# Two attentions of a language-model tower: query quarters, rings of three banks and a new order for the matmuls of a head

## The chip, the cores and the metric

One core of a Trainium2 chip runs the whole program as one launch. The metric is the device time in microseconds (us), the median of several executions. The core's engines run side by side, each on its own queue of instructions in order: TensorE (PE in the profile, with its weight loads as PEld), VectorE (DVE), ScalarE (ACT), GpSimd (POOL) and SyncE (SP), which here only issues DMAs. They meet at semaphores.

## The reference

The program is a tower of a token attention, a second attention with an extra term, a quantised feed-forward, a gated recurrence and six layers of local attention. The change lies in what the first two share. Cut to that (the token attention; the second one has temperature 1 in place of the scale, and adds three more features to the dot products):

```python
q, k, v = (split(q), split(k), split(v))          # 2 batches x 16 heads, 1024 tokens, 16 features a head
scores = jnp.einsum('bhqd,bhkd->bhqk', q, k) * scale
attn = jax.nn.softmax(scores, axis=-1)
ctx = jnp.einsum('bhqk,bhkd->bhqd', attn, v)
```

So there are 32 heads (a batch and a head together, `it` in the kernel) in each of the two attentions, and each has a score matrix of 1024 queries by 1024 keys.

## The kernel before

`softmax_attention` runs twice. `project` makes the queries and keys, splits them into a high and a low half, and writes them to a scratch tensor in HBM; `attend` does all 32 heads; then the output is transposed and projected. Inside `project`, before `attend`, GpSimd fills the value pads and the two rings `qs` and `ks` with constants (L323 to L332), while VectorE makes the scaled query bias `bqs` (L404), which ScalarE waits for before its first copy out of PSUM (L369, L379).

`attend` does a head in six pieces:

- SyncE loads `qs` and `ks` of a head into one of RING slots, 8 DMAs (L473).
- `score_for_max` (L493), 16 matmuls of 128 queries by 512 keys, one PSUM bank each. VectorE takes the maximum of each bank (`maximum`, L610) and then negates and joins them (L614).
- `max_row` (L501) transposes these maxima, 4 one-column transposes for each half of the queries, and ScalarE copies the row into partition 0 of `qs` (`take_row`, L572), so that the next matmuls subtract the maximum by themselves.
- `score` (L509), 16 matmuls of 128 keys by 512 queries; ScalarE takes the exponential of each bank into `probs` (L590).
- `weigh` (L521), in 4 groups a head: 4 matmuls of 32 weight columns by 512 queries, one key tile each, side by side in the four 32-column strips of the array. A half of the queries takes two groups. The four strips hold partial sums over different key tiles.
- ScalarE copies the 128 by 512 result (`take_output`, L578); `sum_groups` (L530), 4 matmuls with a constant matrix, adds the four strips and turns queries onto partitions; VectorE divides by the sums of the exponentials (`finish`, L620, L622).

The order of the work is written out by hand: a step of the PE queue works on the maxima of head `it + 1` and the scores of head `it` in turn, with the other pieces dropped in at fixed places (L544 to L563). The two kinds of matmul each have a ring of two PSUM banks. All engines run 4 steps unrolled, then a loop of 6 turns with 4 steps, then 4 steps unrolled.

## Time and profile before

| What | us |
|---|---|
| Median of 3 runs (4611.0 to 4611.99) | 4611.63 |
| The profiled execution | 4603.94 |
| Its span, first to last instruction | 4601.8 |
| First attention's heads, first maximum matmul to the next stage's first matmul | 123.02 to 617.69 |
| Second attention's heads, the same | 811.78 to 1305.06 |
| Mean granted TensorE clock | 0.962 |

The span is cut into stages in time: the two attentions with their projections fill the first 1310 us or so, and the six layers of local attention most of the rest. The time of a stage is read from its own window, not from the shares of the whole span. A row of a timeline gives the start in us, the duration in us, engine, line, operation and count; rows in one engine may be merged, and the idle time before them stands in brackets with what ended it. Matmuls are pipelined, so the time that one costs is the distance between the starts of neighbours and not its duration.

### The profile page before, as it was taken

To read this page: it belongs to the slowest core of one execution; us is meant where nothing else is said; L and a number is where in the kernel's file an instruction comes from. 1 tells how busy PE (TensorE), PEld (TensorE's weight loads), DVE (VectorE), ACT (ScalarE), POOL (GpSimd) and SP (SyncE) were. 2 spreads that over 40 slices of the span, in tenths; PEclk is the share of its full clock that TensorE was granted. 3 is DMA by queue.
4 is the path that set the end of the run, shared out by engine and by line. 5 is a ranking of instruction groups with operands and counts; after the bars stand their busy time and mean duration, and the time that the engine had idled before them with its cause. 6 is when DMAs were issued, how large, how long until landed. Compare 5 with 4: busy or idle time off the path is not lost. (4 is left out here: it accounts for less than half of the span.)

```text
span 4601.8 us, 97548 instructions
## 1 busy us (share of the span) xinstructions
PE 4219.3 (92%) x32438; PEld 2861.6 (62%) x32440; DVE 3251.8 (71%) x5725; ACT 2756.9 (60%) x7139; POOL 1931.9 (42%) x1276
## 2 busy tenths in 40 slices
PE   4999967999953579999999999999999999999997
PEld 2455543555531347777777777777777777777776
DVE  2677752777766767777777777777777777777775
ACT  1577723577723146666666666666666666666664
POOL 2000010000000056666666666666666666666663
PEclk9899988899977789999999999999999999999999
DMA  4211112211101120011100210011001110111001
GB/s 122 57 41 46 40 27 81 58 43 43 40 19 38 46 85 20 20 34 45 39 17 22 58 39 18 22 49 51 17 20 48 45 26 17 40 39 41 15 22 46
DMA packets 100922, 183.85 MB, mean 40 GB/s; under 512 B 24804, under 2 KB 58240, under 8 KB 100096
## 3 DMA queue, kind: packets, MB, share of 16 engines
q1 hardware_dynamic: 99712, 176.12, 14.3%
q8 instruction: 246, 4.03, 0.4%
q0 software_dynamic: 768, 2.10, 0.2%
q14 instruction: 196, 1.61, 0.1%
HBM read 99.52 MB, written 25.17 MB: 27 GB/s over the span
## 5 line engine op out<-in xcount | busy, mean ns | idle before, releaser
L610 DVE TENSOR_REDUCE maxima<-PS 128x1 f32<-128x512 f32 x1024 | 660.3, 687 | 242.6 <-PE PS L493 232.1
L1426 POOL TENSOR_TENSOR swp<-raw,table 128x512 f32<-128x512 f32 x384 | 481.3, 1274 | 635.8 <-DVE ss L1837 635.6
L1509 PE MATMUL PS<-wqk,xT 128*128 128x512 f32 x1536 | 688.0, 601 | 6.1 <-DMA wqk<-in_L_ffn_Wqkv 4.8
L590 ACT ACTIVATE probs<-PS 128x512 f32<-128x512 f32 x1024 | 551.8, 589 | 223.0 <-PE PS L509 218.5
L1456 POOL TENSOR_TENSOR probs<-probs,prob_recip 128x512 f32<-128x512 f32 x384 | 476.9, 1261 | 431.3 <-DVE prob_recip L1895 431.3
L1766 ACT ACTIVATE probs<-probs,neg 128x128 f32<-128x128 f32 x1536 | 597.1, 392 | 26.6 <-DVE neg L1889 25.1
L1436 POOL TENSOR_TENSOR rinv<-ssm,power 128x32 f32<-128x32 f32 x96 | 528.8, 5508 | 0.0
L493 PE MATMUL PS<-k_stack,q_stack 128*128 128x512 f32 x1024 | 466.6, 459 | 37.4 <-DMA k_stack<-L_attn_qk 17.7
L1509 PEld LDWEIGHTS PS<-wqk,xT 128*128 128x128 f32 x1536 | 284.3, 190 | 337.3 <-issue 254.1
L1612 PE MATMUL PS<-xnT,w 128*128 128x128 f32 x3840 | 477.6, 276 | 0.8 <-DVE hidden L1955 0.8
L482 POOL COPY v_head<-V 128x256 f32 (+1 forms) x64 | 25.4, 403 | 1041.7 <-PE PS L521 859.9
L1612 PEld LDWEIGHTS PS<-xnT,w 128*128 128x128 f32 x3840 | 452.8, 192 | 1.8 <-DVE hidden L1955 1.0
L1837 DVE TENSOR_REDUCE ss<-swp 128x16 f32<-128x1024 f32 x192 | 233.0, 1213 | 303.5 <-ACT swp L1717 303.5
L509 PE MATMUL PS<-q_stack,k_stack 128*128 128x512 f32 x1024 | 406.2, 399 | 2.6 <-ACT q_stack L572 1.4
L1716 ACT ACTIVATE raw<-PS 128x512 f32<-128x512 f32 x384 | 229.5, 598 | 282.6 <-PE PS L1509 278.8
L493 PEld LDWEIGHTS PS<-k_stack,q_stack 128*128 128x128 f32 x1024 | 196.5, 192 | 303.6 <-DVE maxima L610 248.5
L1591 PE MATMUL PS<-wo,oT 128*128 128x256 f32 x1536 | 347.4, 379 | 0.0
L1509 PE MATMUL PS<-wv,xT 128*128 128x512 f32 x768 | 345.8, 593 | 1.2 <-ACT swp L1717 1.2
L1880 DVE TENSOR_TENSOR probs<-PS,maskf 128x512 f32<-128x512 f32 x384 | 261.7, 681 | 101.5 <-PE PS L1553 101.2
L1591 PEld LDWEIGHTS PS<-wo,oT 128*128 128x128 f32 x1536 | 284.4, 190 | 34.7
L1739 ACT ACTIVATE kT<-PS 128x512 f32<-128x512 f32 x192 | 115.2, 600 | 309.5 <-PE PS L1527 309.5
L1901 DVE COPY pT<-PS 128x512 f32<-128x512 f32 x192 | 132.7, 691 | 230.4 <-PE PS L1562 230.1
(231 smaller groups left out, 8567.1 us busy)
## 6 DMA issues: line engine op xcount, KB each, us to landing
V_window<-V SPq DMA_DIRECT2D x180, 256.0 KB, 2.9
wqk<-in_L_ffn_Wqkv SPq DMA_DIRECT2D x12, 1024.0 KB, 6.8
w<-in_L_ffn_W SPq DMA_DIRECT2D x18, 640.0 KB, 4.4
q_stack<-L_tok_qk SPq DMA_DIRECT2D x128, 80.0 KB
k_stack<-L_tok_qk SPq DMA_DIRECT2D x128, 80.0 KB
q_stack<-L_attn_qk SPq DMA_DIRECT2D x128, 80.0 KB
k_stack<-L_attn_qk SPq DMA_DIRECT2D x128, 80.0 KB
wv<-in_L_ffn_Wqkv SPq DMA_DIRECT2D x6, 1024.0 KB, 5.1
```

The costliest lines, as they stand in the source:

```text
L493: pe.matmul(SM(k % 2), qs[:, r, (k // 2) * P:(k // 2 + 1) * P], ks[:, r, (k % 2) * CH:(k % 2 + 1) * CH], start=True, stop=True).then_inc(s ...
L509: pe.matmul(ST(k % 2), ks[:, r, (k % QT) * P:(k % QT + 1) * P], qs[:, r, (k // QT) * CH:(k // QT + 1) * CH], start=True, stop=True).then_i ...
L590: act.activation(probs[:, k % 8, :], ST(k % 2), ACT.Exp).then_inc(exp_done, 1)
L610: dve.tensor_reduce(maxima[:, par, k // 2, k % 2:k % 2 + 1], SM(k % 2), AX.X, ALU.max).then_inc(sm_maxed, 1)
L1426: pool.tensor_tensor(swp[:, w, :, a:a + LD // 2], raw[:, w, :, b:b + LD // 2], table[:, j % 2, 2 + w, a:a + LD // 2].rearrange("p (o d) -> ...
L1436: pool.tensor_tensor(rinv[:, :], ssm[:, :], power[:, :], ALU.pow).then_inc(S["inv_ready"], 1)
L1456: pool.tensor_tensor(view, view, psr[:, 4 * q:4 * q + 4].rearrange("p (h o) -> p h o", o=1) .to_broadcast([P, 4, P]), ALU.mult).then_inc(p ...
L1509: mm = pe.matmul(wide(kind, half, j), xT[:, k, at:at + P], rhs, start=(k == 0), stop=(k == DC - 1))
L1591: mm = pe.matmul(ATT, oT[:, j % 2, k * P:(k + 1) * P], wo[:, k, :], start=(k == 0), stop=(k == PAIRS - 1))
L1612: mm = pe.matmul(bank[:, at * P:(at + 1) * P], w1[:, w, k, f * P:(f + 1) * P], xnT[:, k, :], start=(k == 0), stop=(k == DC - 1), skip_grou ...
L1766: ins_ = act.activation(probs[:, h, :], src, ACT.Exp, bias=neg[:, h:h + 1], accum_out=psum_[:, h:h + 1])
L1880: dve.tensor_tensor(probs[:, 4 * q:4 * q + 4, :], SC(q % 2), maskf[:, int(j % QT == 0), :].rearrange("p (o k) -> p o k", o=1).to_broadcast ...
```

## The change

`attend` is rewritten around the same mathematics:

- `RING` is 6 in place of 4, so `qs` and `ks` have 6 slots each, and `project` fills the larger rings.
- `SM` and `ST` have three PSUM banks each in place of two. A maximum or score matmul waits for the third bank back instead of the second.
- `weigh` gives each of the four strips a quarter of the queries (256) and all key tiles. A burst is 4 key tiles by 4 quarters, 16 matmuls of 32 weight columns by 256 queries; a head has two bursts in place of four groups. Each strip then holds its whole sum, in one bank of 256 columns.
- `sum_groups` goes, and with it the constant `group_sum` and its DMA. `turn_output` takes its place: 2 transposes of 128 by 128.
- The maxima of a head are turned by one 8-column transpose; ScalarE copies 8 by 128 once a head, and SyncE moves it to partition 0 of `qs` with a DMA (`place_row`).
- VectorE does one join, one reciprocal and one multiplication a head in place of two of each.
- The order is new. A step now touches five heads: the maxima of heads `t` and `t - 1`, the scores of `t - 2` and `t - 3`, the weighing of `t - 3` and `t - 4`. There are 36 steps for 32 heads: 6 unrolled, 4 turns of a loop with 6, and 6 more unrolled.

The diff, cut to its core (the removed bodies are those quoted above; the other engines' loops change in the same way):

```diff
-RING = 4
+RING = 6
...
-    GROUP = 4
+    QUARTERS = 4
+    QW = SEQ // QUARTERS
+    BANKS = 3
     vh = c.sb(ctx, "v_head", [P, RING, QT, VW])
-    probs = c.sb(ctx, "probs", [P, 8, CH])
-    maxima = c.sb(ctx, "maxima", [P, 2, QT, 2])
+    probs = c.sb(ctx, "probs", [P, QT, SEQ])
+    maxima = c.sb(ctx, "maxima", [P, QT, HALVES])
     neg_max = c.sb(ctx, "neg_max", [P, 2, QT])
-    partial = c.sb(ctx, "partial", [P, 2, CH])
-    recip = c.sb(ctx, "recip", [P, 2, GROUP])
-    SM, ST, O = (lambda i: c.PS[:, i, :]), (lambda i: c.PS[:, 2 + i, :]), (lambda i: c.PS[:, 4 + i, :])
-    MR, CB = c.PS[0:1, 6, :], c.PS[:, 7, 0:GROUP * VW].rearrange("p (g v) -> p g v", g=GROUP)
+    neg_row = c.sb(ctx, "neg_row", [QT, 2, P], F32R)
+    partial = c.sb(ctx, "partial", [P, 2, QW])
+    recip = c.sb(ctx, "recip", [P, QT])
+    O, CB, MR = c.PS[:, 6, 0:QW], c.PS[:, 7, 0:QW], c.PS[0:QT, 7, QW:QW + P]
+    def SM(r, k):
+        return c.PS[:, (r + k) % BANKS, :]
+    def ST(r, k):
+        return c.PS[:, BANKS + (r + k) % BANKS, :]
...
+    MISC_JOBS = [("row", 1), ("turn", 4)]
+    MISC_TAKEN = {"row": row_taken, "turn": ctx_done}
+    def misc_free(pe, kind, it):
+        at = [k for k, _ in MISC_JOBS].index(kind)
+        t = it + MISC_JOBS[at][1]
+        for back in range(1, 4):
+            k, lag = MISC_JOBS[(at - back) % 2]
+            before = t - (0 if at >= back else (1 if at + 2 >= back else 2)) - lag
+            if not isinstance(it, int) or 0 <= before < ITERS:
+                wait(pe, MISC_TAKEN[k], before + 1)
+                return
+    def over_heads(eng, step, last):
+        for t in range(RING):
+            step(t, t, 0)
+        with eng.Fori(1, ITERS // RING) as turn:
             for u in range(RING):
-                step(turn * RING + u, u)
-        for it in range(ITERS - RING, ITERS):
-            step(it, it % RING)
+                step(turn * RING + u, u, turn)
+        for t in range(ITERS // RING * RING, ITERS + last):
+            step(t, t % RING, t // RING)
+    def stage(t, u, turn, lag):
+        if isinstance(t, int) and not 0 <= t - lag < ITERS:
+            return None
+        return t - lag, (u - lag) % RING, (turn if u >= lag else turn - 1)
...
+            def place_row(h):
+                it, r, turn = h
+                sp.wait_ge(row_taken, it + 1)
+                sp.dma_start(qs[0:1, r, :].rearrange("o (a t) -> o a t", a=QT).bitcast(F32),
+                             neg_row[:, r % 2, :].bitcast(F32)).then_inc(row_loaded[r], 16)
+            def step(t, u, turn):
+                h0, h3 = (stage(t, u, turn, lag) for lag in (0, 3))
+                if h3:
+                    place_row(h3)
+                if h0:
+                    load(h0)
+            over_heads(sp, step, 3)
...
+            def score_for_max(h, k):
+                it, r, turn = h
+                q, half = k // 2, k % 2
                 if k == 0:
-                    pe.wait_ge(loaded[r], (it - r) * (128 // RING) + 128)
-                wait(pe, sm_maxed, m - 1)
-                pe.matmul(SM(k % 2), qs[:, r, (k // 2) * P:(k // 2 + 1) * P], ks[:, r, (k % 2) * CH:(k % 2 + 1) * CH],
+                    pe.wait_ge(loaded[r], 128 * turn + 128)
+                wait(pe, sm_maxed, UNITS * it + k - BANKS + 1)
+                pe.matmul(SM(r, k), qs[:, r, q * P:(q + 1) * P], ks[:, r, half * CH:(half + 1) * CH],
                           start=True, stop=True).then_inc(sm_done, 1)
-            def max_row(it, r, half):
-                pe.wait_ge(neg_ready, 2 * it + half + 1)
-                wait(pe, row_taken, 2 * it + half)
-                for i in range(4):
-                    q = 4 * half + i
-                    mm = pe.transpose(MR[:, i * P:(i + 1) * P], neg_max[:, r % 2, q:q + 1], c.ident[:, :])
-                mm.then_inc(row_done, 1)
-            def score(it, r, k):
-                g = UNITS * it + k
-                if k % QT == 0:
-                    pe.wait_ge(row_taken, 2 * it + k // QT + 1)
-                wait(pe, exp_done, g - 1)
-                pe.matmul(ST(k % 2), ks[:, r, (k % QT) * P:(k % QT + 1) * P], qs[:, r, (k // QT) * CH:(k // QT + 1) * CH],
+            def max_row(h):
+                it, r, turn = h
+                pe.wait_ge(max_ready, it + 1)
+                misc_free(pe, "row", it)
+                pe.transpose(MR, neg_max[:, r % 2, :], c.ident[:, :]).then_inc(row_done, 1)
+            def score(h, k):
+                it, r, turn = h
+                if k == 0:
+                    pe.wait_ge(row_loaded[r], 16 * turn + 16)
+                wait(pe, exp_done, UNITS * it + k - BANKS + 1)
+                pe.matmul(ST(r, k), ks[:, r, (k // 2) * P:(k // 2 + 1) * P], qs[:, r, (k % 2) * CH:(k % 2 + 1) * CH],
                           start=True, stop=True).then_inc(st_done, 1)
-            def weigh(it, r, grp):
-                half = grp // 2
-                pe.wait_ge(exp_done, UNITS * it + 4 * grp + 4)
+            def weigh(h, grp):
+                it, r, turn = h
+                pe.wait_ge(exp_done, UNITS * it + 8 * grp + 8)
                 if grp == 0:
                     pe.wait_ge(v_taken, it + 1)
-                if grp % 2 == 0:
-                    wait(pe, o_taken, 2 * it + half - 1)
-                for j in range(4):
-                    kt = 4 * (grp % 2) + j
-                    mm = pe.matmul(O(half)[VW * j:VW * (j + 1), :], vh[:, r, kt, :], probs[:, 4 * (grp % 2) + j, :],
-                                   start=(grp % 2 == 0), stop=(grp % 2 == 1))
+                    wait(pe, o_taken, it)
+                for kt in range(4 * grp, 4 * grp + 4):
+                    for j in range(QUARTERS):
+                        mm = pe.matmul(O[VW * j:VW * (j + 1), :], vh[:, r, kt, :], probs[:, kt, j * QW:(j + 1) * QW],
+                                       start=(kt == 0), stop=(kt == QT - 1))
                 mm.then_inc(pv_done, 1)
...
+            def turn_output(h):
+                it, r, turn = h
+                pe.wait_ge(o_taken, it + 1)
+                misc_free(pe, "turn", it)
+                for i in range(2):
+                    mm = pe.transpose(CB[:, i * P:(i + 1) * P], partial[:, r % 2, i * P:(i + 1) * P], c.ident[:, :])
+                mm.then_inc(turned, 1)
+            def step(t, u, turn):
+                h0, h1, h2, h3, h4 = (stage(t, u, turn, lag) for lag in (0, 1, 2, 3, 4))
+                if h3:
+                    score(h3, 5)
+                if h1:
+                    score_for_max(h1, 8)
+                if h4:
+                    weigh(h4, 1)
...
+            def take_row(h):
+                it, r, turn = h
+                act.wait_ge(row_done, it + 1)
+                if not isinstance(it, int) or it >= 2:
+                    act.wait_ge(row_loaded[(r - 2) % RING], 16 * (turn if r >= 2 else turn - 1) + 16)
+                act.activation(neg_row[:, r % 2, :], MR, ACT.Copy).then_inc(row_taken, 1)
+            def take_output(h):
+                it, r, turn = h
+                act.wait_ge(pv_done, 2 * it + 2)
+                wait(act, turned, it - 1)
+                act.activation(partial[:, r % 2, :], O, ACT.Copy).then_inc(o_taken, 1)
+            def exponential(h, k):
+                it, r, turn = h
+                act.wait_ge(st_done, UNITS * it + k + 1)
+                if k % 8 == 0:
+                    wait(act, pv_done, 2 * (it - 1) + k // 8 + 1)
+                act.activation(probs[:, k // 2, (k % 2) * CH:(k % 2 + 1) * CH], ST(r, k), ACT.Exp).then_inc(exp_done, 1)
...
+            def maximum(h, k):
+                it, r, turn = h
+                dve.wait_ge(sm_done, UNITS * it + k + 1)
+                if k == 0:
+                    wait(dve, max_ready, it)
+                dve.tensor_reduce(maxima[:, k // 2, k % 2:k % 2 + 1], SM(r, k), AX.X, ALU.max).then_inc(sm_maxed, 1)
+            def row_maxima(h):
+                it, r, turn = h
+                dve.wait_ge(sm_maxed, UNITS * it + UNITS)
+                wait(dve, row_done, it - 1)
+                dve.tensor_reduce(neg_max[:, r % 2, :], maxima[:, :, :], AX.X, ALU.max, negate=True).then_inc(max_ready, 1)
+            def invert(h):
+                it, r, turn = h
+                dve.wait_ge(turned, it + 1)
+                wait(dve, ctx_done, it)
+                view = CB.rearrange("p (c g v) -> p c g v", c=2, g=QUARTERS)
+                dve.reciprocal(recip[:, :].rearrange("p (c g o) -> p c g o", c=2, g=QUARTERS), view[:, :, :, HD:HD + 1]).then_inc(ctx_recip, 1)
+            def finish(h):
+                it, r, turn = h
+                dve.wait_ge(ctx_recip, it + 1)
+                view = CB.rearrange("p (c g v) -> p c g v", c=2, g=QUARTERS)
+                out = context[:, :, bass.ds(it * HD, HD)].rearrange("p (g c) d -> p c g d", c=2)
+                by = recip[:, :].rearrange("p (c g o) -> p c g o", c=2, g=QUARTERS).to_broadcast([P, 2, QUARTERS, HD])
+                dve.tensor_tensor(out, view[:, :, :, 0:HD], by, ALU.mult).then_inc(ctx_done, 1)
...
```

What stands in PE's queue before, from the middle of a head in the unrolled start (L493 is a maximum matmul, L509 a score, L521 a weighing, L530 the sum over strips, L501 the transposes of maxima):

```order
L521 MATMUL PS<-probs,v_head 32x512 [waits exp_done_64]
L521 MATMUL PS<-probs,v_head 32x512 x3
L493 MATMUL PS<-k_stack,q_stack 128x512 [waits sm_maxed_59]
L509 MATMUL PS<-q_stack,k_stack 128x512 [waits exp_done_64,row_taken_62]
L493 MATMUL PS<-k_stack,q_stack 128x512 [waits sm_maxed_59]
L509 MATMUL PS<-q_stack,k_stack 128x512 [waits exp_done_64]
L530 MATMUL PS<-group_sum,partial 128x32 [waits ctx_done_69,o_taken_66]
L530 MATMUL PS<-group_sum,partial 128x32 x3
```

and now, in the first step that has all pieces (L539 is a maximum matmul, L553 a score, L564 a weighing burst):

```order
L539 MATMUL PS<-k_stack,q_stack 128x512 [waits sm_maxed_67]
L564 MATMUL PS<-probs,v_head 32x256 [waits exp_done_72]
L564 MATMUL PS<-probs,v_head 32x256 x15
L539 MATMUL PS<-k_stack,q_stack 128x512 [waits sm_maxed_67]
L553 MATMUL PS<-q_stack,k_stack 128x512 [waits exp_done_72]
L539 MATMUL PS<-k_stack,q_stack 128x512 [waits sm_maxed_67]
L553 MATMUL PS<-q_stack,k_stack 128x512 [waits exp_done_72] x2
```

The weighing matmuls of a head are 32 in place of 16, each half as wide, and they stand in two runs of 16 instead of four runs of 4.

The transposes of the maxima and the score that needs the row, now on PE (L546 is the one transpose, `row_loaded` the DMA's semaphore):

```order
L553 MATMUL PS<-q_stack,k_stack 128x512 [waits exp_done_72,row_loaded1_61]
L546 MATMUL PS<-ident,neg_max 8x128 [waits row_taken_70,max_ready_68]
L553 MATMUL PS<-q_stack,k_stack 128x512 [waits exp_done_72]
L539 MATMUL PS<-k_stack,q_stack 128x512 [waits sm_maxed_67]
```

The score waits here for the row of one head, and the transpose right behind it makes the row of the next, so the row has nearly a whole step to arrive. Before, the row of a head was copied in two halves inside the head's own step.

On VectorE, one head before (L610 the maxima, L614 the join, L620 and L622 the division):

```order
L610 TENSOR_REDUCE maxima<-PS 128x1 [waits row_done_61,sm_done_58]
L610 TENSOR_REDUCE maxima<-PS 128x1 [waits sm_done_58]
L620 RECIPROCAL recip<-PS 128x4 [waits sum_done_67]
L622 TENSOR_TENSOR context<-PS,recip 128x4x16 [waits ctx_recip_68]
L610 TENSOR_REDUCE maxima<-PS 128x1 [waits sm_done_58] x6
L614 TENSOR_REDUCE neg_max<-maxima 128x4 [waits sm_maxed_59]
```

and now (L705, L711, L718 and L726 in the same roles):

```order
L711 TENSOR_REDUCE neg_max<-maxima 128x8 [waits row_done_69,sm_maxed_67]
L705 TENSOR_REDUCE maxima<-PS 128x1 [waits max_ready_68,sm_done_66]
L705 TENSOR_REDUCE maxima<-PS 128x1 [waits sm_done_66] x5
L718 RECIPROCAL recip<-PS 128x8 [waits turned_75]
L705 TENSOR_REDUCE maxima<-PS 128x1 [waits sm_done_66] x2
L726 TENSOR_TENSOR context<-PS,recip 128x2x4x16 [waits ctx_recip_76]
```

The rows of before are half a head, those of now the first half of a step; the reciprocal waits for the two transposes of `turn_output`, with two maxima between it and the multiplication.

## Rows read from the trace of the kernel before

**Rows 1.** Window of 440 us: busy of PE, PEld, DVE, ACT, POOL, clock, DMA share, GB/s

```profile
160.00:600.00 440.00, 440.00 (x2594) 249.81 (x2592) 331.92 (x649) 310.72 (x590) 10.89 (x27) 1.00 0.16 41
```

**Rows 2.** Timeline of PE, first attention, half a head

```profile
401.08 0.40 PE L509 MATMUL PS<-q_stack,k_stack 128*128 128x512 f32 x1
401.40 1.07 PE L521 MATMUL PS<-probs,v_head 128*32 128x512 f32 x8
...
402.74 0.40 PE L509 MATMUL PS<-q_stack,k_stack 128*128 128x512 f32 x1
...
403.20 0.40 PE L509 MATMUL PS<-q_stack,k_stack 128*128 128x512 f32 x1
403.44 0.60 PE L501 MATMUL PS<-ident,neg_max 128*1 128x128 f32 x4
...
404.11 0.39 PE L509 MATMUL PS<-q_stack,k_stack 128*128 128x512 f32 x1
...
406.73 0.40 PE L509 MATMUL PS<-q_stack,k_stack 128*128 128x512 f32 x1
406.97 0.97 PE L530 MATMUL PS<-group_sum,partial 128*128 128x32 f32 x8
...
408.09 0.39 PE L509 MATMUL PS<-q_stack,k_stack 128*128 128x512 f32 x1
...
408.87 1.06 PE L521 MATMUL PS<-probs,v_head 128*32 128x512 f32 x8
```

**Rows 3.** Groups of instructions: busy us, mean ns of one, then idle before

```profile
L610 DVE TENSOR_REDUCE maxima<-PS 128x1 f32<-128x512 f32 x1024 | 660.3, 687 | 242.6 <-PE PS L493 232.1
L1591 PE MATMUL PS<-wo,oT 128*128 128x256 f32 x1536 | 347.4, 379 | 0.0
```

**Rows 4.** Timeline of PE in the local layers: 256-column matmuls back to back

```profile
2499.26 2.32 PE L1591 MATMUL PS<-wo,oT 128*128 128x256 f32 x10
```

**Rows 5.** Timeline of PEld: weight loads of one weighing group

```profile
401.40 0.16 PEld L521 LDWEIGHTS PS<-probs,v_head 128*32 128x32 f32 x8 [0.36 <-issue]
```

**Rows 6.** Timeline of PE in the local layers: strips of 64 columns, and transposes

```profile
2511.54 0.60 PE L1562 MATMUL PS<-ident,probs 128*128 128x128 f32 x4
...
2512.35 0.29 PE L1580 MATMUL PS<-pT,V_window 128*64 128x64 f32 x4
2512.47 0.29 PE L1580 MATMUL PS<-pT,V 128*64 128x64 f32 x4
```

**Rows 7.** Timeline of DVE, half a head

```profile
402.43 0.23 DVE L622 TENSOR_TENSOR context<-PS,recip 128x64 f32 x1
...
406.47 1.29 DVE L610 TENSOR_REDUCE maxima<-PS 128x1 f32<-128x512 f32 x2 [0.86 <-PE PS L493]
407.79 0.16 DVE L614 TENSOR_REDUCE neg_max<-maxima 128x4 f32<-128x8 f32 x1
```

**Rows 8.** Timeline of ACT, two exponentials

```profile
403.25 1.09 ACT L590 ACTIVATE probs<-PS 128x512 f32<-128x512 f32 x2
```

**Rows 9.** Timeline of PE: start and end of the heads of each attention

```profile
123.02 1.22 PE L493 MATMUL PS<-k_stack,q_stack 128*128 128x512 f32 x2 [16.57 <-DMA k_stack<-L_tok_qk]
124.60 1.39 PE L493 MATMUL PS<-k_stack,q_stack 128*128 128x512 f32 x2 [0.36 <-DVE maxima L610]
...
617.69 1.09 PE L165 MATMUL PS<-ident,context 128*128 128x128 f32 x4 [0.80 <-PEq L464]
...
811.78 1.22 PE L493 MATMUL PS<-k_stack,q_stack 128*128 128x512 f32 x2 [17.74 <-DMA k_stack<-L_attn_qk]
...
1305.06 1.17 PE L165 MATMUL PS<-ident,context 128*128 128x128 f32 x9 [0.80 <-PEq L464]
```

**Rows 10.** Timeline of POOL, DVE and ACT in the first projection

```profile
53.45 3.50 POOL L332 MEMSET k_stack<- 128x4096 f32 x1
...
46.48 10.50 DVE L404 TENSOR_SCALAR bqs<-bqk,factor 128x2 f32<-128x2 f32 x1 [2.26 <-POOL factor L326]
...
57.02 0.78 ACT L379 ACTIVATE whole<-PS,bqs,factor 128x512 f32<-128x512 f32 x1 [9.15 <-DVE bqs L404]
```

250 lines of the change are left out of this document (133 added, 117 removed).

## The prediction

> **What bounds the kernel now.** I read a window from the middle of the first attention first, then PE's timeline in it, and only then the other engines. In the window [rows 1] PE is busy for all of its 440 us at full clock (1.00), VectorE for 332 and ScalarE for 311, and DMA for 0.16. A busy PE proves little, since its records overlap, so the timeline has to say whether it ever waits. A weighing group starts at 401.40 and the one two places on, half a head later, at 408.87: 7.47 us a half, 14.94 a head. Priced by the starts of neighbours [rows 2]: two matmuls of scores or maxima lie between 402.74 and 403.20, so 0.23 each and 3.7 for the 16 of a half. From 401.08 to 402.74 stand two of them and a weighing group: 1.66 less 0.46 is 1.20, twice a half, 2.40. The four transposes of maxima: 403.20 to 404.11, less 0.46, 0.45. The sum over strips: 406.73 to 408.09, less 0.46, 0.90. Together 7.45 of 7.47. PE waits for nobody; a head costs what PE's queue costs, and every us taken out of that queue is one gained until VectorE or the rings get in the way.
>
> **The weighing.** A head now has 32 matmuls of 256 queries instead of 16 of 512, the same columns in all. The same moving size runs elsewhere: ten records of 256 columns take 2.32 us with 0.38 the mean of one [rows 3, 4], so (2.32 - 0.38) / 9 = 0.216 a record, and an fp32 matmul has two records. If the four strips run side by side, a burst is 4 key tiles x 2 x 0.216 = 1.73. The old group at that rate streams 2 x 0.43 = 0.86 of its 1.20; the other 0.34 is getting into and out of the strips, and is now paid twice a head instead of four times. So 2 x (1.73 + 0.34) = 4.14 against 4.80. The new part is that a strip needs fresh weights every 0.216 instead of every 0.43. Eight loads of a group occupy 0.16 in all, the second four beginning while the first matmuls run [rows 5], 0.08 a round; and in the local layers strips of 64 columns pass four matmul records in 0.12, each with a load of its own [rows 6]. I take the loads as hidden. Bounds: 1.73 below, and above, with every round showing its 0.08, 1.73 + 0.64 = 2.4 plus the 0.34.
>
> The Trainium skill (TensorE: Matmul & The Clock Gate, Measured speedup vs the span model) says that weight loads overlap with matmuls in flight only when the row group differs; all four strips here use all 128 rows, so by it the loads show and the upper bound holds. The trace disagrees: a score with its own 128-column load, on all rows too, still follows its neighbour after 0.23 [rows 2]. I keep a small chance for it below.
>
> **Transposes and the sum.** The four one-column transposes cost 0.45, 0.11 each [rows 2], and four full 128 by 128 transposes take the same 0.60 from first start to last end as those do [rows 2, 6], so I price both at 0.11. Before: 2 x (0.45 + 0.90) = 2.70 a head. Now one and two: 0.33. Upper bound 0.90, if the two transposes cost as much as the old sum.
>
> PE's queue for a head is then 32 x 0.23 + 4.14 + 0.33 = 11.8 to 11.9 (half-head prices are rounded), against 14.9.
>
> **VectorE and ScalarE.** Two maxima take 1.29 with 0.69 the mean of one, so the second starts 0.60 after the first [rows 3, 7]. Sixteen are 9.7; the join, of 0.16 [rows 7], waits for the last maximum and so costs some 0.3; a reciprocal and a multiplication, now once a head, some 0.5 (0.23 for the half-sized multiplication). That is 10.5, under PE's 11.9. Two exponentials take 1.09 [rows 8], 0.55 each at most, 8.8 a head, and two copies of 256 and 128 columns follow in place of four of 512: under 10.
>
> **The rings.** What decides between 11.9 and more is whether three banks carry VectorE over a burst and let PE run ahead after it. The nearest row: after a group of 1.20, with two banks, VectorE had been idle 0.86 [rows 7]. A burst is 0.87 longer and there is one more bank, worth 0.60: 1.13 idle a burst, so VectorE's own cycle would be 10.5 + 2 x 1.13 = 12.8 if the rings were always empty behind a burst. PE issues a maximum every 0.46 and VectorE takes one in 0.60, so after a burst PE gains 0.14 a pair and meets the end of the ring only after some four or five; then it waits a little. There are 7 pairs after one burst and 9 after the other. Between 11.9 and 12.8 I take 12.3 a head, nearer PE's sum because that sum met the kernel before to 0.02 us.
>
> **The row by DMA.** The row of a head is fetched nearly a step, some 11 us, before its score needs it, and SyncE's queue holds only the loads of a head three steps away ahead of it. I cost it at nothing. GpSimd's copy of the values waits for the second burst of a head six back; nothing waits for that.
>
> **Start and end.** Each attention's heads took 617.69 - 123.02 = 494.7 and 1305.06 - 811.78 = 493.3 [rows 9], 988.0 together. Now: steps 0 to 2 hold only 40 maxima (and five scores). At the start a pair of maxima took 1.58 (124.60 - 123.02, [rows 9]), 0.79 each, with PE waiting on VectorE's two banks; with three I take VectorE's own 0.60: 24 us, and 1 for joins (32 by the old rate). Then 29 full steps. Then the drain: step 32 has 24 matmuls and both bursts, 10; step 33 sixteen exponentials, 9; step 34 eleven and a burst, 8; step 35 a burst, a copy, two transposes and a division, 4: 31. Two more as an allowance for the first step that has scores in full. 25 + 29 x 12.3 + 31 + 2 = 415. Two attentions: 830, so 158 less.
>
> **What the larger rings cost.** GpSimd's fill of one ring takes 3.50 for 4096 columns [rows 10], and both grow by half: 3.5 us an attention. It is not hidden: VectorE's tiny scaling of the bias, 128 by 2, began at 46.48 and took 10.50, to within 0.05 of the end of the last fill (53.45 + 3.50), and ScalarE's first copy waits for it, idle 9.15 [rows 10]. Everything in the projection hangs on that copy. So 2 x 3.5 = 7 us come back. The Trainium skill (SBUF — State Buffer, SBUF: two separate sides) calls the port pair of VectorE and GpSimd an exclusive lock that the loser waits out. By that rule the wait would grow by the whole 3.5, and the row's 10.50 agrees.
>
> **Sum.** 158 - 7 = 151 off the profiled execution's 4603.9: 4453. The median of the runs shown is 7.7 above that execution; on its scale 4460.
>
> **Rivals.** (a) My forecast, PE's queue with small waits: 4460; its own range is 4437 (11.9 a head: 0.4 less in each of the 58 full steps) to 4489 (12.8). Chance 0.50. (b) The rings couple the engines: VectorE pays its 1.13 at each burst, and beside that waits about 0.5 for the two transposes of the output, which stand late in PE's step. 13.3 a head, 1.0 x 58 more: 4518. For it speak the 0.86 idle now and the reciprocal in the middle of eight maxima; against it PE's slack over VectorE. 0.30. (c) The page's rule on loads: eight rounds each show 0.08 more, 1.3 a head: 4535. Against it the 0.23 of a score. 0.05. (d) Slower: the strips don't stay side by side when 16 matmuls follow each other, and each of the seven changes of weights within a burst pays the entry of 0.34 again: 2.4 a burst, 4.8 a head, 278 us: 4738. It decides from 151 / 58 = 2.6 a head, 0.19 a change. No row shows two rounds with 32-column loads and 256 columns behind each other; rows 6 speak against it with 64-column strips. 0.08. (e) No change of note: the row's DMA or the loads arrive late, and a step waits its 14.9 out on them; about 4615. The loads keep a ring and DMA is busy 0.16 [rows 1]. 0.07, shared out between the smaller gains, no change and loss.
>
> **The numbers.** Faster by over 0.2% (9 us, about what can be told from no change): (a), (b), (c) and part of (e), 0.88. Within 0.2%: 0.03. Slower: 0.09. The range, 4425 to 4540, leaves out (d) and (e) and a few us below (a), where the fills stay hidden and the start is short.
>
> **What would show it.** Right: the weighing bursts two a head, 12.3 us apart from one head's first to the next's; the start of what follows a burst 2.1 after it; VectorE's scaling of the bias 3.5 longer; the rest of the program unmoved. Wrong by (b): PE's weight loads for the maxima idle on VectorE for more than 0.5 a head. Wrong by (c) or (d): bursts of 2.7 or more. Wrong by (e): the score after a row waits for the DMA.

## The result, and the profile after

| | before | after |
|---|---|---|
| Median, us | 4611.32 (4608.69 to 4611.99, 4 runs) | 4441.75 (4439.11 to 4443.88, 4 runs) |
| Ratio, 95% interval | | 0.9633 (0.9616 to 0.965) |
| Profiled execution, us | 4603.94 | 4443.18 |
| First attention's heads, us | 494.7 | 536.39 - 128.03 = 408.4 |
| Second attention's heads, us | 493.3 | 1143.60 - 735.01 = 408.6 |

3.7% faster; the forecast was 4460. The heads of both attentions give 988.0 - 817.0 = 171.0 us and the rest of the program takes back 10.2. The window of the heads, with the columns of [rows 1], and then the waits between 200 and 480 us (engine, line and what it waited for: total us, times, longest), both of the kernel after:

```profile
180.00:480.00 300.00, 300.00 (x2473) 192.58 (x2472) 255.10 (x475) 212.12 (x450) 9.67 (x24) 1.00 0.22 55
```

```profile
DVE maxima L705 <- PE PS L539: 40.9, 47, 1.0
...
PEld PS L553 <- ACT probs L669: 17.3, 90, 0.2
...
PEld PS L539 <- DVE maxima L705: 9.9, 24, 0.4
PEld PS L539 <- issue: 9.5, 23, 0.4
```

No single wait is longer than 1.0 us in these rows, and no row of PE's own queue waits for a transfer. The last two rows belong together: behind each of a head's two bursts the next weight load idles 0.4, at one burst put down to VectorE and at the other to nothing. PE's timeline for one head shows what the waits are worth (start us, duration us; a maximum matmul is L539 now, a score L553, a burst L564, the transpose of the maxima L546, those of the output L573):

```profile
301.79 0.40 PE L539 MATMUL PS<-k_stack,q_stack 128*128 128x512 f32 x1
302.12 1.93 PE L564 MATMUL PS<-probs,v_head 128*32 128x256 f32 x32
303.98 0.50 PE L539 MATMUL PS<-k_stack,q_stack 128*128 128x512 f32 x1
304.32 0.39 PE L553 MATMUL PS<-q_stack,k_stack 128*128 128x512 f32 x1
...
305.71 0.40 PE L553 MATMUL PS<-q_stack,k_stack 128*128 128x512 f32 x1
305.94 0.27 PE L546 MATMUL PS<-ident,neg_max 128*8 128x128 f32 x1
305.97 0.48 PE L553 MATMUL PS<-q_stack,k_stack 128*128 128x512 f32 x1
306.29 0.40 PE L539 MATMUL PS<-k_stack,q_stack 128*128 128x512 f32 x1
...
307.46 0.41 PE L553 MATMUL PS<-q_stack,k_stack 128*128 128x512 f32 x1
307.71 0.38 PE L573 MATMUL PS<-ident,partial 128*128 128x128 f32 x2
307.84 0.48 PE L539 MATMUL PS<-k_stack,q_stack 128*128 128x512 f32 x1
308.16 0.40 PE L553 MATMUL PS<-q_stack,k_stack 128*128 128x512 f32 x1
...
308.72 1.93 PE L564 MATMUL PS<-probs,v_head 128*32 128x256 f32 x32
...
308.72 1.45 PEld L564 LDWEIGHTS PS<-probs,v_head 128*32 128x32 f32 x32 [0.29 <-ACT probs L669]
```

Read by starts, as [rows 2] were: six steps from 304.32 to 305.71 are 1.39, 0.23 each, as before. A burst costs 304.32 - 301.79 = 2.53 less two steps, 2.06. The row's transpose costs 306.29 - 305.71 = 0.58 less two steps, 0.11; the two of the output 308.16 - 307.46 = 0.70 less two, 0.24. Over the window the bursts start 6.61 and 5.42 apart in turn, 12.03 a head. I call the 6.61 from the burst in the middle of a step (behind tile 15 of the maxima) to the one near the start of the next (behind tile 8) the long stretch; PE's sum in it is 18 x 0.233 + 2.06 + 0.35 = 6.60. The short stretch has 14 x 0.233 + 2.06 = 5.32 in 5.42.

VectorE in the same head (idle time in brackets, L705 a maximum, L711 the join, L718 and L726 the division), where [rows 7] had 0.86 idle behind a group of 1.20:

```profile
303.41 0.17 DVE L711 TENSOR_REDUCE neg_max<-maxima 128x8 f32<-128x16 f32 x1
304.52 3.68 DVE L705 TENSOR_REDUCE maxima<-PS 128x1 f32<-128x512 f32 x6 [0.93 <-PE PS L539]
308.12 0.21 DVE L718 RECIPROCAL recip<-PS 128x8 f32<-128x8 f32 x1
308.25 1.26 DVE L705 TENSOR_REDUCE maxima<-PS 128x1 f32<-128x512 f32 x2
309.43 0.28 DVE L726 TENSOR_TENSOR context<-PS,recip 128x128 f32 x1
...
311.12 4.28 DVE L705 TENSOR_REDUCE maxima<-PS 128x1 f32<-128x512 f32 x7 [0.82 <-PE PS L539]
```

Between bursts it never stops. It idles 0.82 and 0.93 behind the two bursts, and 12.03 less that is 10.3 of work. So two limits may hold this kernel, and they read almost the same: PE's sum, 11.92, and VectorE's work plus what a burst starves it of. The second comes to 12.03 by construction, since work and idleness together always fill the head, so it proves nothing by itself. The experiments turn on which of the two holds.

A third engine leaves a trace in the short stretch. Three score matmuls a head wait there with their weight load for a bank that ScalarE still reads, and PE's steps at them are 0.52 for two, 0.25 and 0.27 where they are 0.23 elsewhere (starts 312.31, 312.83, 313.07, 313.32, 313.54, 313.81); that is about the 0.1 between 5.32 and 5.42. One of the three:

```profile
312.49 0.19 PEld L553 LDWEIGHTS PS<-q_stack,k_stack 128*128 128x128 f32 x1 [0.22 <-ACT probs L669]
```

Start and end of the heads, and the fills ahead of them, which answer to [rows 9] and [rows 10]:

```profile
128.03 0.79 PE L539 MATMUL PS<-k_stack,q_stack 128*128 128x512 f32 x1 [17.26 <-DMA k_stack<-L_tok_qk]
...
536.39 3.87 PE L164 MATMUL PS<-ident,context 128*128 128x128 f32 x32 [0.90 <-PEq L492]
...
735.01 0.79 PE L539 MATMUL PS<-k_stack,q_stack 128*128 128x512 f32 x1 [17.76 <-DMA k_stack<-L_attn_qk]
...
1143.60 0.52 PE L164 MATMUL PS<-ident,context 128*128 128x128 f32 x3 [0.89 <-PEq L492]
...
50.77 5.21 POOL L330 MEMSET q_stack<- 128x6144 f32 x1
55.92 5.21 POOL L331 MEMSET k_stack<- 128x6144 f32 x1
...
47.25 13.91 DVE L403 TENSOR_SCALAR bqs<-bqk,factor 128x2 f32<-128x2 f32 x1 [2.26 <-POOL factor L325]
...
588.52 15.69 DVE L403 TENSOR_SCALAR bqs<-bqk,factor 128x2 f32<-128x2 f32 x1
```

The scaling went from 10.50 to 13.91 us, and still ends with the last fill (55.92 + 5.21 = 61.13, against 61.16). The heads start 5.0 later in the first attention, the stretch from the first attention's end to the second's start is 4.5 longer (194.1, now 198.6), and the rest grows by 0.9.

### The profile page after: what moved, and what is told of

The parts are those of the page before. It is cut to its first block and busy times, and to the rows that moved or that the text cites. A ratio compares the mean times of both kernels' runs of the same rounds, so it can differ in the third digit from the quotient of the medians.

```text
span 4441.2 us, 98171 instructions
## 1 busy us (share of the span) xinstructions
PE 4048.9 (91%) x33142; PEld 2813.6 (63%) x33144; DVE 3197.5 (72%) x5533; ACT 2627.5 (59%) x7011; POOL 1930.9 (43%) x1276
## 5 line engine op out<-in xcount | busy, mean ns | idle before, releaser
L705 DVE TENSOR_REDUCE maxima<-PS 128x1 f32<-128x512 f32 x1024 | 631.6, 680 | 129.9 <-PE PS L539 129.5
L669 ACT ACTIVATE probs<-PS 128x512 f32<-128x512 f32 x1024 | 519.2, 602 | 153.8 <-PE PS L553 153.3
L539 PE MATMUL PS<-k_stack,q_stack 128*128 128x512 f32 x1024 | 428.1, 438 | 36.4 <-DMA k_stack<-L_attn_qk 17.8
L553 PE MATMUL PS<-q_stack,k_stack 128*128 128x512 f32 x1024 | 392.1, 413 | 2.2 <-ACT probs L669 2.2
L1882 ACT ACTIVATION_READ_ACCUMULATOR probs<-probs,neg 128x1 f32 x1536 | 286.9, 187 | 0.0
```

The source lines that it names most:

```text
L539: pe.matmul(SM(r, k), qs[:, r, q * P:(q + 1) * P], ks[:, r, half * CH:(half + 1) * CH], start=True, stop=True).then_inc(sm_done, 1)
L553: pe.matmul(ST(r, k), ks[:, r, (k // 2) * P:(k // 2 + 1) * P], qs[:, r, (k % 2) * CH:(k % 2 + 1) * CH], start=True, stop=True).then_inc(st ...
L669: act.activation(probs[:, k // 2, (k % 2) * CH:(k % 2 + 1) * CH], ST(r, k), ACT.Exp).then_inc(exp_done, 1)
L705: dve.tensor_reduce(maxima[:, k // 2, k % 2:k % 2 + 1], SM(r, k), AX.X, ALU.max).then_inc(sm_maxed, 1)
L1882: ins_ = act.activation(probs[:, h, :], src, ACT.Exp, bias=neg[:, h:h + 1], accum_out=psum_[:, h:h + 1])
```

## The experiments

Theories. A: TensorE's queue of 11.92 sets the head, and waits add little. C: VectorE sets it, through the three banks of its ring. Where a later run asks for one stretch or one ring, A is called Q and C is called V; S is ScalarE through the exponentials' ring, E both engines level. L: the fills hold VectorE's bias scaling until the last one ends; W: something else sets its end; R: moved fills hold VectorE elsewhere instead. Medians are compared with 4441.8 for the kernel after; "heads" is the mean time of one attention's heads in the profile, 408.5 for it (first maximum matmul to the next stage's first matmul; in the experiments, to the last multiplication of the output, 408.15 for it).

**Is the burst what I priced?** Each burst is cut in two with a score or maximum matmul between the parts:

```
-                for kt in range(4 * grp, 4 * grp + 4):
+                for kt in range(4 * grp + 2 * part, 4 * grp + 2 * part + 2):
...
                 if h1:
                     score_for_max(h1, 9)
+                if h4:
+                    weigh(h4, 1, 1)
...
                 if h0:
                     score_for_max(h0, 0)
+                if h3:
+                    weigh(h3, 0, 1)
```

> The kernel after, with each burst of 16 weighing matmuls cut into two of 8, with one maximum matmul between them: four bursts of two key tiles a head in place of two bursts of four. Theory A (PE's queue sets a head, and each burst costs 0.33 us for entering and leaving the strips): 2 x 0.33 us x 62 heads or so, 41 us more, 4483 us. Theory C (VectorE's idle time behind long bursts sets a head): shorter bursts are kinder to the rings, so less than 10 us more, or less than the kernel after.

4482.82 us (4480.28 to 4486.68), ratio to before 0.9728 (0.9712 to 0.9744): 41.1 slower than after. PE's timeline:

```profile
309.86 1.07 PE L565 MATMUL PS<-probs,v_head 128*32 128x256 f32 x16
310.86 0.49 PE L539 MATMUL PS<-k_stack,q_stack 128*128 128x512 f32 x1
311.28 1.07 PE L565 MATMUL PS<-probs,v_head 128*32 128x256 f32 x16
```

A part and the matmul behind it take 311.28 - 309.86 = 1.42. Two key tiles are four records of 0.216 in each strip, 0.87 with the strips side by side; a step is 0.23; 0.32 is left for entering and leaving. The price of 0.34 an entry holds, and with it rival (d) falls: seven changes of weights inside a burst cost nothing.

**One PE cost doubled in the long stretch.**

```
-                for i in range(2):
+                for i in (0, 1, 0, 1):
                     mm = pe.transpose(CB[:, i * P:(i + 1) * P], partial[...
```

> The kernel after, with the two 128 by 128 transposes of the output done twice into the same place, 4 in place of 2 a head. Theory A (PE's queue sets a head): two more transposes of 0.11 us for each of 64 heads, 14 us more, 4456 us. Theory C (the rings and VectorE set a head, PE has air): 0 to 3 us more, 4442 to 4445 us.

4455.64 us (4452.54 to 4456.46), ratio 0.9667 (0.9651 to 0.9683): 13.9 slower. The long stretch is 6.81 instead of 6.61, the short one still 5.42. 0.20 of the 0.24 shows, as A says. Alone this doesn't decide, because the two transposes more also hold VectorE, whose reciprocal waits for them. In the kernel after they end at 307.71 + 0.38 = 308.09, just as VectorE is through its six maxima; here VectorE is through at about 305.54 + 6 x 0.60 = 309.14 and the transposes end at 308.72 + 0.60 = 309.32:

```profile
305.54 3.68 DVE L705 TENSOR_REDUCE maxima<-PS 128x1 f32<-128x512 f32 x6 [0.94 <-PE PS L539]
309.35 0.21 DVE L718 RECIPROCAL recip<-PS 128x8 f32<-128x8 f32 x1
```

So VectorE's cycle grew by 0.2 too. That PE is full in the long stretch is shown by its starts, 6.60 by the sum in 6.61, more than by this run.

**One VectorE cost added, in the short stretch and then in the long one.** A maximum more a head over one bank (128 by 512), at tile 12, and in the second kernel at tile 4:

```
+                if k == 12:
+                    wait(dve, spare_done, it)
+                    dve.tensor_reduce(spare[:, 0:1], SM(r, k), AX.X, ALU.max).then_inc(spare_done, 1)
```

> The kernel after, with one more maximum of a bank on VectorE for each head, into a spare tile, between the twelfth and the thirteenth of a head: 0.60 us more VectorE work a head, nothing more on PE. Theory A (PE's queue of 11.9 us sets a head of 12.02, VectorE has about 1 us of air, but the rings hold only three banks of it): 0 to 0.3 us a head more, 4442 to 4460 us. Theory C (VectorE's cycle sets a head): the whole 0.6 us a head, 38 us more, 4480 us.

> The changed kernel with one more maximum over a 128x256 score tile on VectorE in every head (its result goes to a spare tile and is not used), as in the run before it of this kind, but at key tile 4 of the scan, in the stretch of 6.6 us from the burst in the middle of a step to the burst at the start of the next, and not at key tile 12, in the stretch of 5.4 us behind it, where it cost 37.7 us. Theory A, each stretch has its own bound: in the longer stretch TensorE's queue of 18 matmuls, a burst and three transposes is full (6.6 by the sum of its steps, 6.61 measured) and VectorE has nine maxima, the row's maximum and the two operations on the output there, 6.1 us, with some 0.5 to spare; the 0.61 us of another maximum are hidden but for 0 to 0.1 a head: 4442 to 4450, and the shorter stretch stays at 5.42. Theory C, VectorE through the three-bank ring sets the pace all round: +0.6 a head as at key tile 12, 4480.

At tile 12: 4479.47 us (4478.37 to 4480.32), ratio 0.9718 (0.9702 to 0.9734), 37.7 slower; short stretch 5.97, long 6.60. A, as I held it then, missed by 19 us or more and C was right. I tried to save A by giving each stretch its own bound, and the run at tile 4 contradicts that too: 4477.92 us (4475.96 to 4478.46), ratio 0.9718 (0.9703 to 0.9733), 36.1 slower; long stretch 7.16, short 5.42. The first row is PE's timeline at tile 4, the others VectorE's:

```profile
303.25 0.50 PE L540 MATMUL PS<-k_stack,q_stack 128*128 128x512 f32 x1 [0.17 <-DVE maxima L709]
...
299.52 2.48 DVE L709 TENSOR_REDUCE maxima<-PS 128x1 f32<-128x512 f32 x4 [0.94 <-PE PS L540]
301.92 0.68 DVE L708 TENSOR_REDUCE spare<-PS 128x1 f32<-128x512 f32 x1
...
306.67 4.27 DVE L709 TENSOR_REDUCE maxima<-PS 128x1 f32<-128x512 f32 x7 [0.82 <-PE PS L540]
```

The idleness behind the bursts stays at 0.94 and 0.82: it isn't slack that more work could fill. It is the time of a burst that three banks don't bridge, so it belongs to VectorE's cycle. Each stretch grew by 0.55 for a maximum of 0.60. So in the kernel after VectorE was some 0.05 short of setting either stretch: about 5.37 and 6.56, 11.93 a head, an estimate from these two runs, beside PE's 11.92. Neither engine has room worth the name in the long stretch.

**A PE cost in the short stretch.**

```
                 wait(pe, sm_maxed, UNITS * it + k - BANKS + 1)
+                if k == 12:
+                    pe.matmul(SM(r, k), qs[:, r, q * P:(q + 1) * P], ks[:, r, half * CH:(half + 1) * CH],
+                              start=True, stop=True)
```

> The changed kernel, in which TensorE computes the score tile of key tile 12 of the scan twice into the same bank, one matmul more of 0.23 us a head, in the stretch of 5.42 us from the burst at the start of a step to the one in its middle, where TensorE's own steps sum to 5.32. Twice as many output transposes in the other stretch cost 13.9 us, 0.22 a head, and one maximum more cost 38 us in either stretch. Theory Q, TensorE's queue binds here too: +0.23 a head, 14 to 15 us, 4456. Theory V, in this stretch VectorE through its ring of three banks is 0.1 behind TensorE, and the first 0.1 of the matmul fills that wait: +0.13 a head, 8 us, 4450.

4455.3 us (4453.53 to 4457.98), ratio 0.9667 (0.9654 to 0.968): 13.5 slower, which is Q's number. The profile says otherwise: the bursts of the short stretch lie 5.57 apart, not 5.42, the long stretch is unchanged, and the heads grow by 4.8 and 4.1 us, 8.9 in all, which is the size that V gave. What is over lies between the attentions in the profiled run (2.9) and behind the second (1.1), where nothing was changed; from the last multiplication of the one to the first maximum matmul of the other, the nine profiles in which the fills stand as in the kernel after, this one among them, read 196.6 to 201.9. V's mechanism does not hold, though. With PE's waits for ScalarE's and for VectorE's banks in the same 280 us, and VectorE behind the burst in the middle of a step:

```profile
PEld PS L556 <- ACT probs L672: 9.0, 50, 0.2
...
PEld PS L542 <- DVE maxima L708: 9.5, 23, 0.4
...
305.95 3.68 DVE L708 TENSOR_REDUCE maxima<-PS 128x1 f32<-128x512 f32 x6 [1.09 <-PE PS L542]
```

The scores' waits for ScalarE fell from 90 to 50 and from 17.3 us to 9.0, those for VectorE stayed (9.9, now 9.5), and VectorE's idleness grew from 0.93 to 1.09, by what the stretch grew. So the added matmul went into the time that PE had spent waiting for ScalarE, and VectorE had a little room in the short stretch. No run here changes ScalarE's work, so its share of the 0.1 rests on these rows.

**Which banks carry it?** First two banks for either ring, with the order and the bursts of the kernel after:

```
-    BANKS = 3
+    BANKS = 2
...
-        return c.PS[:, (r + k) % BANKS, :]
+        return c.PS[:, k % BANKS, :]
...
-        return c.PS[:, BANKS + (r + k) % BANKS, :]
+        return c.PS[:, 3 + k % BANKS, :]
```

> The kernel after, with two PSUM banks in each of the two rings in place of three; the order and the bursts of 16 stay. Theory A (PE's queue of 11.9 us sets a head, and three banks are what lets it): with two banks VectorE is idle 0.86 us behind a burst of 1.2 in the kernel before, so 0.87 more behind a burst of 2.07: 10.5 + 2 x 1.73 = 14.0 us a head, or a little more, since the order has two matmuls of one kind behind each other: about 2.0 to 2.4 us x 58 more, 4557 to 4580 us. Theory B (the gain is the shorter PE queue alone, the third bank is not needed): 12.0 us a head, 4442 us.

4639.08 us (4636.9 to 4640.68), ratio 1.0064 (1.0048 to 1.0081): 197 slower than after, slower even than before, and 59 above the top of what I expected. Then one ring at a time, here the maxima's four and the exponentials' two (the second kernel has two and three, by the same places):

```
-        return c.PS[:, (r + k) % BANKS, :]
+        return c.PS[:, k % 4, :]
...
-        return c.PS[:, BANKS + (r + k) % BANKS, :]
+        return c.PS[:, 4 + k % 2, :]
...
-                wait(pe, sm_maxed, UNITS * it + k - BANKS + 1)
+                wait(pe, sm_maxed, UNITS * it + k - 4 + 1)
...
-                wait(pe, exp_done, UNITS * it + k - BANKS + 1)
+                wait(pe, exp_done, UNITS * it + k - 2 + 1)
```

> The changed kernel with the six score banks shared out otherwise: four for the tiles whose maxima VectorE takes, two for the tiles whose exponentials ScalarE takes (three and three in the changed kernel; two and two made it 197 us slower). What is open is which of the two rings that loss came from, and whether VectorE's 0.8 to 0.9 us of idleness behind each burst is what holds the head at 12.02. Theory V, the maxima's ring: with four banks VectorE has 0.6 us more to do during a burst, its idleness falls to about 0.3, and TensorE's queue alone sets the head at 11.9: 4435 to 4442. Theory S, the exponentials' ring: two banks make each score wait for the exponential two tiles back (some 0.4 for the matmul, 0.5 for the exponential and 0.1 between them, against a pitch of 0.47 in TensorE's order), and the waits behind the bursts come on top; then most of the 197 us are here: 4600 to 4640. Both alike: 4530 to 4560.

> The changed kernel with two banks for the tiles whose maxima VectorE takes and three for the exponentials' (two and two made it 197 us slower). Theory V, the maxima's ring carries the loss: VectorE idles 1.3 to 1.5 us behind each burst instead of 0.82 and 0.93, and TensorE waits for it at the other tiles: 4600 to 4640. Theory S, the exponentials' ring carries it: 4442 to 4480, of which 1.2 us a head less idleness hidden would be the most. Both alike: 4530 to 4560.

| Banks, maxima / exponentials | Median, us | Ratio to before, 95% | Long and short stretch, us | Heads, us |
|---|---|---|---|---|
| 3 / 3, after | 4441.75 | 0.9633 (0.9616 to 0.965) | 6.61, 5.42 | 408.2 |
| 4 / 2 | 4563.71 | 0.9904 (0.9889 to 0.992) | 7.63, 6.32 | 468.6 |
| 2 / 3 | 4582.81 | 0.9942 (0.9927 to 0.9957) | 8.10, 6.16 | 479.5 |
| 2 / 2 | 4639.08 | 1.0064 (1.0048 to 1.0081) | 8.47, 6.51 | 504.8 |

Neither V nor S: each ring alone, one bank short, costs 122 or 141 us, and both short cost 197. "Both alike" was right in kind, and 4 to 23 us low. With four and two, the scores' waits for ScalarE went from 17.3 to 71.4 us in 280, and VectorE still idled up to 1.4 behind a burst. Three and two was not run, so what the fourth bank was worth to the maxima is not shown. In PE's order the two kinds alternate, so a wait for either stops both. What it looks like with two banks, PE first (a gap that begins with a bank that isn't free) and then VectorE, whose idleness behind a burst is 1.3 to 1.5:

```profile
306.14 0.40 PE L553 MATMUL PS<-q_stack,k_stack 128*128 128x512 f32 x1
307.04 0.50 PE L539 MATMUL PS<-k_stack,q_stack 128*128 128x512 f32 x1 [0.50 <-DVE maxima L705]
...
301.32 2.57 DVE L705 TENSOR_REDUCE maxima<-PS 128x1 f32<-128x512 f32 x4 [1.30 <-PE PS L539]
...
306.19 0.21 DVE L718 RECIPROCAL recip<-PS 128x8 f32<-128x8 f32 x1 [0.57 <-PE PS L573]
```

So in this order the shorter weighing and the lost transposes, 3 us a head on paper, are worth nothing with two banks in both rings, and 26 or 45 us of the 167 with two in one of them. The bursts with the order of before were not tried.

**The fills.** In the kernel before, the key ring's fill done twice:

```
+            pool.wait_ge(pads_set, 4)
+            pool.memset(ks[:, :, :].bitcast(F32), 0.0).then_inc(pads_set, 1)
```

> The kernel before, whose fill of the key ring is done twice, one behind the other (3.5 us more on GpSimd in each attention, zeros over zeros, nothing else changed). It puts the one cost that the change has ahead of its heads into the old kernel. Theory L, fills back to back hold VectorE's bias scaling until the last of them ends: scaling 14.0 instead of 10.50 us, each attention's heads 3.5 later, +7: 4616. Theory W, something else sets the end of the scaling, and the larger fills are hidden: 4609 within 2.

4607.33 us (4604.74 to 4612.65), ratio 0.9999 (0.999 to 1.0008): no change. L's 4616 missed and W's number was met, but not for W's reason, as the kernel after and the next run show. POOL and VectorE:

```profile
54.15 3.50 POOL L332 MEMSET k_stack<- 128x4096 f32 x1
57.71 3.51 POOL L334 MEMSET k_stack<- 128x4096 f32 x1
...
47.18 10.50 DVE L406 TENSOR_SCALAR bqs<-bqk,factor 128x2 f32<-128x2 f32 x1 [2.26 <-POOL factor L326]
```

The added wait left 57.71 - 57.65 = 0.06 us between the fills, and VectorE ended at 57.68, inside it. Elsewhere a fill starts 0.05 or so before the one ahead of it ends (55.92 against 50.77 + 5.21 above). So a gap of 0.06 is enough, and VectorE is not held until the fills are over. The second attention of this run repeats it (gap at 683.87, scaling over at 683.90). And in the kernel after, the fills put behind the scaling:

```
+            pool.wait_ge(factor_ready, 1)
             pool.memset(V[:, :, :, HD:HD + 1], 1.0).then_inc(pads_set, 1)
```

> The changed kernel, where GpSimd waits for VectorE's factor (what both attentions compute ahead of their bias scaling) before it begins the fills of the value pads and of the two operand rings. Theory L, the fills hold VectorE: its scaling of the query bias, 128x2, took 13.91 us beside the fills and ended with them; without the overlap it is done in under 1 us and ScalarE's stage starts earlier: 4 us in the first attention, which then waits for its parameters' transfers, and up to 13 in the second: 4424 to 4435. Theory R, the fills are only moved: they then hold VectorE's first evictions of the projections by as much, and the time stays at 4442 (within 2). Theory W: what waited was the transfer of the bias, not the scaling: no change either, and the scaling still ends at about 61.

4420.99 us (4419.64 to 4423.15), ratio 0.9595 (0.9582 to 0.9609): 20.8 faster than after, and the fastest kernel of the study. VectorE, GpSimd's two small fills that stay ahead of the scaling, and then PE where the heads start:

```profile
46.40 0.23 DVE L404 TENSOR_SCALAR bqs<-bqk,factor 128x2 f32<-128x2 f32 x1 [2.26 <-POOL factor L325]
...
582.65 0.80 DVE L404 TENSOR_SCALAR bqs<-bqk,factor 128x2 f32<-128x2 f32 x1
...
582.48 0.94 POOL L322 MEMSET edge<- 32x1024 f32 x1 [12.92 <-POOLq L156]
583.38 0.96 POOL L323 MEMSET edge<- 32x1024 f32 x1
...
121.91 0.79 PE L540 MATMUL PS<-k_stack,q_stack 128*128 128x512 f32 x1 [16.76 <-DMA k_stack<-L_tok_qk]
...
712.93 0.79 PE L540 MATMUL PS<-k_stack,q_stack 128*128 128x512 f32 x1 [17.74 <-DMA k_stack<-L_attn_qk]
```

13.91 us became 0.23, and 15.69 became 0.80. W falls with that. R falls too: VectorE's next instructions, 128 by 512 with both sources in SBUF, take 0.69 beside the moved fills, as they do without. The first attention starts only 6.1 earlier, since ScalarE then waits longer for a transfer instead (12.38 at its third pair of copies, not 4.64); the second starts 22.1 earlier, 16 of it its own. My 4424 was for 4 and 13. The 0.80 leaves the rule of the gap open: that scaling ended at 583.45, with the first of the two fills (583.42), although the second begins at 583.38 and leaves none. The second attentions of the two runs below show the same. In the kernel after, the scaling stood before the same two fills and did not get in between them. What decides there is not shown.

The third way, the fills in the stage before:

```
-    to_feature_major(c, lambda t, k: c.X[:, t, k * P:(k + 1) * P], XT)
+    to_feature_major(c, lambda t, k: c.X[:, t, k * P:(k + 1) * P], XT, meanwhile=fill)
```

> The changed kernel with GpSimd's fills moved ahead, into the stage that transposes the source to feature-major, where GpSimd is idle and VectorE copies half of the tiles out of PSUM. Theory L, the fills hold VectorE where it reads and writes in its faster mode or takes the port they share: if the copies of the transposed tiles are held as the bias scaling was, that stage gets up to 14 us longer and the scaling 13 shorter, no gain: 4435 to 4445. If copies whose source is PSUM are not held, the whole 13 us come out of the second attention and some 4 or more out of the first: 4420 to 4430. Theory W, the bias's transfer sets the end of the scaling: 4442.

4439.83 us (4438.06 to 4444.31), ratio 0.9638 (0.9625 to 0.9652): no gain worth the name, within the range for held copies by luck, for the reason was another. VectorE's copies out of PSUM in that stage keep their 0.69 beside a fill, and the scaling takes 0.23. But its factor is also made by GpSimd, now behind the fills; in the second attention, which has its factor already, VectorE waits 7.06 for the stage to end, and the stage ends with the fills:

```profile
53.96 0.23 DVE L409 TENSOR_SCALAR bqs<-bqk,factor 128x2 f32<-128x2 f32 x1 [9.35 <-POOL factor L336]
```

**Can the split be bettered?** The later fills, and the first burst of a step one scan matmul later, which makes the maxima ten and six:

```
-                if h4:
-                    weigh(h4, 1)
                 if h1:
                     score_for_max(h1, 9)
+                if h4:
+                    weigh(h4, 1)
```

> The changed kernel with GpSimd's fills behind the bias scaling (alone this took 4421.0 us) and the burst at the start of a step one scan matmul later, behind key tile 9 and not 8, so that the 16 maxima divide as ten and six over the two stretches and not nine and seven. Theory E, TensorE's queue and VectorE with its idleness of 0.8 to 0.9 at each burst are level in both stretches: what one stretch gains (0.6 on VectorE, 0.23 on TensorE) the other loses, by the slower of the two, and moving VectorE's work to the stretch where TensorE has less room gives nothing or loses up to 0.37 a head: 4421 to 4443. Theory G, the 0.1 a head that TensorE waits in the shorter stretch goes: 4415.

4450.74 us (4445.36 to 4452.39), ratio 0.9654 (0.9641 to 0.9667): 29.7 slower than with the later fills alone, 8 above E's range; G fell. The long stretch is 7.28 and the short 5.18. The long one pays VectorE's maximum and a little more (+0.67; VectorE idles 1.12 to 1.14 behind the moved burst, not 0.82), the short one gives back only PE's matmul (-0.24). 12.8 us an attention are in the heads, the other 4 in the rest. Of the two splits tried, nine and seven has the engines level in both stretches.

## Why the prediction was right

The sign and the place held, and so did the main mechanism, a head that costs what PE's shorter queue costs. The forecast was 18 us too high, and VectorE's part in it was misread. By its own terms:

- **PE's queue.** Score step 0.23, as taken. A burst 2.06, forecast 1.73 + 0.34 = 2.07, with the entry shown by the cut bursts. Transposes 0.35, forecast 0.33. The sum is 11.92, forecast 11.8 to 11.9. Rival (c), loads that show, falls: the 32 loads of a burst, 1.45, lie beside the 1.93 of its matmuls, and the rule of the Trainium skill's page on TensorE that I had weighed (TensorE: Matmul & The Clock Gate, The mechanism) is not what this trace does. The prediction named another section of that page; the rule stands in this one.
- **VectorE.** 10.5 forecast, 10.3 measured, as the head less the idleness.
- **The rings: the term that was mis-sized.** I had 1.13 us idle behind each burst, and from it 12.8 as the upper end, and took 12.3. Measured are 0.82 and 0.93. The bank's worth of 0.60 stands roughly (1.3 to 1.5 idle with two banks in both rings, 0.82 and 0.93 with three). The half that failed is that a burst 0.87 longer starves VectorE by 0.87 more: the kernel with two banks shows 1.30 to 1.49 where before had 0.86, so 0.5 or so. Why only so much is not settled. I also treated 12.8 as a case in which the rings are empty and 11.9 as one in which they aren't; the added maxima show that VectorE's cycle with its idleness, some 11.93, lies within 0.1 of the head, and any longer VectorE would set it. With that read rightly, the sum would have been 12.0. For the same reason "PE waits a little, behind four or five pairs" was right in size (0.1 a head) and wrong in what it stood for: I thought VectorE had 1.4 us a head to spare, and it has 0.1; and the waits that make up PE's 0.1 are put down to ScalarE's banks, a ring that the forecast did not look at. That PE's sum and VectorE's cycle came out level is luck: the forecast priced one of them and took the other for slack.
- **Rival (b)** was right that VectorE's idleness at each burst belongs to its cycle, and had too large a price (1.13 for 0.82 and 0.93). Its sign did not show: weight loads for the maxima waited 9.9 us in 280, 0.4 a head, and as much stands behind the other burst without VectorE; the reciprocal waited for nothing in the middle of the attention. It is what the kernel becomes with two banks in a ring (0.57 at the reciprocal, 1.3 to 1.5 at each burst).
- **The row by DMA.** Nothing waited for it, in the waits above or at the score behind it.
- **Start and end.** 415 forecast, 408.5 measured. 29 steps at 12.05 (12.03 and the loop's turn, 0.17 every sixth head) instead of 12.3 are 7.2 less, so the 58 for filling and draining came out as 59. Both attentions: 13 of the 18 us.
- **The larger fills.** +3.5 each forecast, +3.4 measured on the scaling in both attentions (13.91 against 10.50; in the second 15.69 against 12.28). In all 10.2 came back outside the heads and not 7; the first attention's fills also began 0.8 later, and the rest, under 3 us, I can't place. The stretch between the attentions alone differs by 5 us between profiles of the same code. The reason, a lock, was right and incomplete: the exclusive lock of the Trainium skill (SBUF — State Buffer, SBUF: two separate sides) fits the 13.91 and 0.23 of the same instruction. But the page speaks of a lock held for one instruction, and here one VectorE instruction was passed over by several fills in a row, so the whole 3.5 did not follow from it; a gap of 0.06 us let the loser in, and in three runs it got in without one. The larger miss is one of reading: I priced the 3.5 that the change adds and passed over the 10.50 already there, of which one added wait gives back more than 20 us.
- The other 5 of the 18 us: I had put the median 7.7 above the profiled execution, and it is 1.4 below it (4441.75 and 4443.18), 9 in all, less the 3 that came back beyond the 7, and less the rounding of 4460.6 to 4460. The size of the miss is thus partly scatter.

## What to carry to other kernels

An engine that idles only behind another's long, unbroken piece of work is not slack: add to its work the idleness that the banks can't bridge before calling it free, and compare that sum with the other engine's queue. Before shortening a queue, count the banks between it and its consumers; here the new order with two banks in both rings lost all that it won, and with two in one ring most of what it won. A tiny instruction that lasts as long as its neighbour's fill is a wait written down as work; move the fill behind it.

## What the runs showed of the hardware

- The 32 weight loads of 32 columns in a burst, four in each round of 0.216 us, stay hidden behind fp32 matmuls of 256 columns: the burst costs 2.06, its matmuls 1.73 of it. Entering and leaving the strips costs 0.32 to 0.34, whether the burst is 0.87 or 1.73 long.
- The first matmul after a burst, a transpose or a wait has a duration of 0.50 or 0.48 and its follower starts 0.32 to 0.34 later, not 0.23, so by these rows a wait of PE costs 0.1 more than it lasts (304.32 - 303.98 behind a burst, 308.16 - 307.84 behind transposes). In the kernel with two banks such rows stand at every second or third matmul.
- GpSimd's fills back to back held a VectorE instruction of 128 by 2 elements, source and result in SBUF, for 13.91 and 15.69 us; it ran in 0.23 without them, and slipped through a gap of 0.06. In the second attention of three runs it was let in at the end of a small fill with no gap in the rows (0.79 and 0.80 us), so a gap is enough and not shown to be needed. Copies with the source in PSUM (0.69 in the stage before) and 128 by 512 subtractions with both sources in SBUF (0.69) were not held.
